# Two-part fp32r products turned into single plain fp32 products, and expert weights kept in SBUF

## The chip, the core and the metric

The kernel runs on one core of a Trainium2 chip. The core has a matrix engine (TensorE, PE in the profile, with its weight loads shown apart as PEld), VectorE (DVE), ScalarE (ACT), GpSimd (POOL), and SyncE (SP), which here only issues DMAs. The metric is the device time of one execution in microseconds (us).

## The reference, cut to what matters

x has 16 sequences of 256 tokens, each of 256 numbers. An attention layer and then a mixture of experts are added to it.

```python
xn = ln(x, g_norm); q = xn @ Wq                # 16 heads of 64
kv = xn @ Wkv                                   # one key, one value, shared by the heads
q, k = l2norm(q) * q_scale, l2norm(k) * k_scale # a null key and value stand ahead
attn = softmax(q @ k.T * 8 + relative_bias + causal + mask)
x = x + ln((attn @ v) @ Wout, g_out)
logits = (x @ wt.T + cond @ wg.T) / 2           # router over 8 experts, the best 2 weighted
y = sum over 8 experts: w[e] * ((leaky(x @ w_gate[e]) * (x @ w_up[e])) @ w_down[e])
y = y + (leaky(x @ sw_gate) * (x @ sw_up)) @ sw_down   # 2 shared blocks of 128
x = x + y
```

## The kernel before, in words

The work goes in eight rounds of 512 tokens (four tiles of 128). Round r does the attention of its tokens and, woven into it, the experts of round r - 1; after round 7 the experts of round 7 run alone. The order on every engine is written out by hand, and semaphores with counts (`need`) join the engines. Round 0 and rounds 1 to 6 (a loop) and 7 are built by the same function `attention(r, moe, following)`; in round 0 `moe` is None.

On PE a round goes like this. `turn_x1` turns the attention's output of the round before; `q_half` makes the queries (16 products of 512 columns a round, four of them ahead of time in `q_first`); `logits` makes the router's; then `gate` and `up` make 20 units of two products each (ten blocks: two shared ones and eight experts). Three of the ten blocks come before the scores, seven within them. Then 21 steps follow, each with a `score`, a `down` product of a block, a `gate` or an `up`, a `turn` of probabilities and a `value`. At the end come `turn_x` for the following round, the output product with `Wout`, and within it `keys(following)`.

Six kinds of products are made exact by parts. A number is split into a leading part, rounded to the type fp32r by a copy, and the rest, by a subtraction; `products` (lines 65 to 71) then issues three fp32r matmuls for each product of two split operands. So are made the keys' (`keys`, L1339), queries' (`q_half`, L1352), gate's and up's (`gate_up`, L1608, and in the last experts `block_half`, L1572) and the output's (with `Wout` and `oT`). The router's (`logits`, L1583) has its two weight parts side by side in one operand and two more matmuls. The other products (`down`, L1641; `score`, L1511; `value`, L1547; the null column) are plain fp32 ones already.

The parts of the activations are made in each round: ACT copies the leading part from PSUM and DVE subtracts (`keys` and `x1_parts`). The parts of the weights are made once. `Wall` (queries' and keys' columns) is split in the prologue. The gate and up weights of the ten blocks are split in round 0, one block a step from step 6 on: SP loads a block into the ring `H`, ACT makes its leading part (L740), DVE the rest (L1071), and SP writes both to an HBM scratch `wexp`. In each round all ten blocks are read again from `wexp` into `Wgu`, a ring of three blocks, by `load_weights` on SP's queue, each when the `up` that last used its place is done.

Keys' products have 256 columns, of which 144 are used (64 key, 64 value, 16 for the null key's scores): the rest are columns of the queries that stand beside them in `Wall`.

The gate and up products have one PSUM bank (`psG`) within the rounds, so a `gate` waits for DVE's `hidden` of the block before, and `up` for ACT's copy of the gate.

Of the kernel before, what the change touches and what calls it, by code (L numbers as in the profile page):

```python
# [17 lines left out]
P = 128  # L18
# [8 lines left out]
TOK = 512  # L27
# [13 lines left out]
FIRST_WEIGHTS = (1, 2, 0)  # L41
H_RING = 3
W_RING = 3
# [8 lines left out]
SPLIT_AT = 6  # L52
# [67 lines left out]
def attention_moe(nc, x, condT, condR, mask, wq, wkv, wout, wgu, wdown, wt, wgT, gnorm,  # L120
# [3 lines left out]
    wexp = nc.dram_tensor("wexp", (BLOCKS, P, 2, 2, KC, P), F32, kind="Internal")  # L124
# [4 lines left out]
    with ExitStack() as ctx:  # L129
# [13 lines left out]
        Wall = [sb(f"Wall_{part}", [P, KC, KVN + HEADS * DH], F32R) for part in PARTS]  # L143
        KV0, Q0 = 0, KVN
        WtP = sb("WtP", [P, KC, 2 * E], F32R)
        I2 = sb("I2", [2 * E, E])[:]
# [17 lines left out]
        xnT = [sb(f"xnT_{part}", [P, KC, TOK], F32R) for part in PARTS]  # L164
# [43 lines left out]
        x1T = [sb(f"x1T_{part}", [P, KC, TOK], F32R) for part in PARTS]  # L208
        Wgu = sb("Wgu", [P, W_RING, 2, 2, KC, P], F32R)
# [3 lines left out]
        LT = sb("LT", [2 * E, TOK])[:]  # L213
        WT = LT[0:E, :]
# [40 lines left out]
        wnull = misc[:, 128:160]  # L255
# [9 lines left out]
        Wq_in = work[:, 0:KC * HEADS * DH].rearrange("p (c k) -> p c k", c=KC)  # L265
# [3 lines left out]
        Wkvn_in = work[:, 4096:4096 + KC * KVN].rearrange("p (c k) -> p c k", c=KC)  # L269
# [17 lines left out]
        def logit_bank(last):  # L287

            return psY[0:2 * E, 1, :] if last else psO[0:2 * E, :]
# [41 lines left out]
        wraw_in = [events(f"wraw_in{i}", 0) for i in range(H_RING)]  # L331
        lead_done = events("lead_done", 0)
        parts_done = events("parts_done", 0)
        parts_out = [events(f"parts_out{i}", 0) for i in range(W_RING)]
# [7 lines left out]
        wgu_ld = [events(f"wgu_ld{i}", 16 * len(range(i, BLOCKS, W_RING))) for i in range(W_RING)]  # L342
# [3 lines left out]
        xnT_v = events("xnT_v", 3)  # L346
# [14 lines left out]
        x1T_v = events("x1T_v", KC)  # L361
# [16 lines left out]
        x1T_a = events("x1T_a", KC)  # L378
# [28 lines left out]
        u_ps = events("u_ps", BLOCKS, W_RING)  # L407
# [7 lines left out]
        V_MASK, V_VAR0, V_NSS, V_SILU0, V_ACT0, V_CX, V_KV, V_WALL = 2, 19, 22, 27, 29, 34, 44, 46  # L415
        V_VAR1, V_SILU1, V_ACT1, V_REL, V_RB, V_WOUT = 52, 55, 56, 58, 59, 61
# [23 lines left out]
        def _(sp):  # L440
# [6 lines left out]
            sp.dma_start(Wkvn_in[:, :, 0:2 * DH], wkv).then_inc(ld_kv.sem, 16)  # L447
# [32 lines left out]
            def load_weights(m, k):  # L480

                former = k - W_RING if k >= W_RING else max(range(k, BLOCKS, W_RING)) - BLOCKS
                need(sp, u_ps, m, former + 1)
                stand(sp, waited_sp)
                sp.dma_start(Wgu[:, k % W_RING].bitcast(F32), wexp.ap()[ORDER[k]]).then_inc(wgu_ld[k % W_RING].sem, 16)

            def experts(m):
                for k in range(W_RING, 2 * W_RING):
                    load_weights(m, k)

# [6 lines left out]
                for e in range(E):  # L497
                    if e >= WB_RING:

                        need(sp, hw_done, m, e - WB_RING + 1)  # L500
                        stand(sp, waited_sp)
                    sp.dma_start(Wb[:, e % WB_RING, :], wscr.ap()[e:e + 1, :].to_broadcast([P, TOK])) \
                        .then_inc(wb_in[e % WB_RING].sem, 16)
                    if 1 <= e <= BLOCKS - 2 * W_RING:
                        load_weights(m, 2 * W_RING + e - 1)
# [21 lines left out]
            for e in range(BLOCKS + 2):  # L527
                if e < BLOCKS:
                    if e >= H_RING:
                        sp.wait_ge(parts_done.sem, e - H_RING + 1)  # L530
                    sp.dma_start(H[:, e % H_RING, :], wgu[e].rearrange("p w c m -> p (w c m)")) \
                        .then_inc(wraw_in[e % H_RING].sem, 16)
                if e >= 2:
                    sp.wait_ge(parts_done.sem, e - 1)
                    sp.dma_start(wexp.ap()[e - 2], Wgu[:, (e - 2) % W_RING].bitcast(F32)) \
                        .then_inc(parts_out[(e - 2) % W_RING].sem, 16)
            sp.wait_ge(pre_v.sem, V_WOUT)
            sp.dma_start(xres[:], x_t[0]).then_inc(xres_in.sem, 16)
            for i in range(W_RING):
                sp.wait_ge(parts_out[i].sem, 16 * len(range(i, BLOCKS, W_RING)))  # L540
            for k in FIRST_WEIGHTS:
                load_weights(0, k)
            with sp.Fori(1, ROUNDS - 1) as r:
                load_norm_x(r + 1)
                load_round(r)
                experts(r - 1)
                for k in FIRST_WEIGHTS:
                    load_weights(r, k)
                store(r - 1)
            load_round(ROUNDS - 1)  # L550
            experts(ROUNDS - 2)
            for k in FIRST_WEIGHTS:
                load_weights(ROUNDS - 1, k)
# [80 lines left out]
        def _(act):  # L634

            act.dma_start(xin[:], x_t[0]).then_inc(xin_in.sem, 16)
            act.dma_start(Wq_in, wq).then_inc(ld_q.sem, 16)
            act.wait_ge(ld_kv.sem, 32)
            for c in range(KC):
                act.activation(Wkvn_in[:, c, 0:2 * DH], Wkvn_in[:, c, 0:2 * DH], ACT.Copy,  # L640
# [4 lines left out]
            for c in range(KC):  # L645
                act.activation(Wq_in[:, c, :], Wq_in[:, c, :], ACT.Copy, scale=gn[:, c:c + 1]) \
# [12 lines left out]
            for c in range(KC):  # L659
                act.wait_ge(w_scaled.sem, KC + c + 1)  # L660
                act.activation(Wall[0][:, c, Q0:], Wq_in[:, c, :], ACT.Copy).then_inc(w_lead.sem, 1)
            positions_turned(1)

            def keys(r, first=False):

                need(act, xnT_ps, r, 1)
                act.activation(xnT[0][:, 0, :], psT[:, 0, :], ACT.Copy).then_inc(xnT_a.sem, 1)
                if first:
                    need(act, xnT_ps, r, 2)
                    act.activation(xnT[0][:, 1, :], psT[:, 1, :], ACT.Copy).then_inc(xnT_v.sem, 1)  # L670
# [10 lines left out]
            def attention(r, moe, following):  # L681
# [35 lines left out]
                for n in range(ALL + VALUE_LAG):  # L717
# [16 lines left out]
                    if moe is None and 0 <= n - SPLIT_AT < BLOCKS:  # L734

                        e = n - SPLIT_AT
                        act.wait_ge(wraw_in[e % H_RING].sem, 16 * (e // H_RING + 1))
                        if e >= W_RING:
                            act.wait_ge(parts_out[e % W_RING].sem, 16 * (e // W_RING))
                        act.activation(Wgu[:, e % W_RING, 0], H[:, e % H_RING, :].rearrange(  # L740
                            "p (w c m) -> p w c m", w=2, c=KC), ACT.Copy).then_inc(lead_done.sem, 1)
# [36 lines left out]
            def route(m):  # L778
                for c, bank in ((0, psG), (1, psO)):
                    need(act, x1T_ps, m, c + 1)  # L780
                    act.activation(x1T[0][:, c, :], bank[:], ACT.Copy).then_inc(x1T_a.sem, 1)

            def route_half(m, half):
                for c in range(KC):
                    need(act, x1T_ps, m, KC * half + c + 1)
                    act.activation(x1T[0][:, c, half_tokens(half)], psT[:, c, half_tokens(half)], ACT.Copy) \
                        .then_inc(x1T_a.sem, 1)
# [39 lines left out]
        def _(dve):  # L827
# [69 lines left out]
            def null_columns():  # L897

                dve.wait_ge(w_scaled.sem, 2 * KC)
                for c in range(KC):  # L900
                    pre(dve.tensor_tensor(wprod, Wq_in[:, c, :].rearrange("p (h d) -> p h d", h=HEADS),
                                          knull.unsqueeze(1).to_broadcast([P, HEADS, DH]), ALU.mult))
                    pre(dve.tensor_reduce(wnull[:, c * HEADS:(c + 1) * HEADS], wprod, AX, ALU.add))
                pre(dve.tensor_copy(Wkvn_in[:, :, 2 * DH:], wnull.rearrange("p (c h) -> p c h", c=KC)))

# [827 lines left out]
```

## Time and profile before

| | |
|---|---|
| time, median of 3 runs | 1060.24 us (1060.23 to 1061.74) |
| the profiled execution: its own time | 1064.17 us |
| its span in the profile | 1062.4 us |
| mean granted TensorE clock | 0.994 |
| busy: PE, PEld | 1014.6 us (96%), 815.3 us (77%) |
| busy: DVE, ACT, POOL | 707.4, 526.5, 437.0 us |
| moved by DMA | 87.68 MB, 83 GB/s in the mean |

Busy times are of the profiled execution. The profile models the end of a matmul, and matmuls overlap in the pipe, so what one matmul costs in a row of equal ones is the distance from one start to the next, and not the duration that its row shows. In the timelines a row is: start, duration, engine, line, operation, output and inputs, shapes, count, and in brackets the idle time before it with what ended it. A shape "128*128 128x512" is that of the weights and that of the streamed operand. A plain fp32 matmul of the kernel shows as two PE instructions.

### The profile page before, as it was taken

What the parts mean: (1) busy time and instruction counts of PE and PEld (TensorE: products, weight loads), DVE (VectorE), ACT (ScalarE), POOL (GpSimd) and SP (SyncE); (2) the same over time, 40 slices, a digit from 0 to 9 for tenths busy, and PEclk for the clock granted to TensorE, in tenths of its full rate; (3) what the DMA queues carried; (4) which work ended last, traced back from release to release, by engine and by line L of the source; (5) the groups of instructions that cost most, each with busy time, mean ns of one, the idle gap of its engine ahead of it and who ended that gap; (6) DMA issues with size and microseconds to landing.
All of it is one profiled execution on the core that took longest, in us unless ns stands there. A gap on an engine that the chain in (4) does not pass through costs nothing.

```text
span 1062.4 us, 21427 instructions
## 1 busy us (share of the span) xinstructions
PE 1014.6 (96%) x6788; PEld 815.3 (77%) x6788; DVE 707.4 (67%) x2457; ACT 526.5 (50%) x1564; POOL 437.0 (41%) x422
## 2 busy tenths in 40 slices
PE   3887999999999999999999999999999999999998
PEld 2665877778777887778777787777877788777877
DVE  8789577665867558665676647676576755856543
ACT  3488346651565435663456614665246643565220
POOL 1634154441554333642535515454245534444212
PEclk9899999999999999999999999999999999999999
DMA  5316414112132013311132212311123211232043
GB/s 198 80 54 215 151 60 122 53 66 63 61 110 90 28 55 101 100 61 61 43 118 72 71 42 79 112 65 46 62 66 113 82 41 41 84 106 71 20 138 102
DMA packets 40996, 87.68 MB, mean 83 GB/s; under 512 B 4192, under 2 KB 19040, under 8 KB 40624
## 3 DMA queue, kind: packets, MB, share of 16 engines
q1 hardware_dynamic: 39920, 83.57, 24.5%
q10 hardware_dynamic: 960, 2.62, 0.7%
q8 instruction: 66, 1.08, 0.4%
q14 instruction: 50, 0.41, 0.1%
HBM read 76.57 MB, written 9.60 MB: 81 GB/s over the span
## 4 chain that ended last, share of the span: by engine, by line
PE 75%; DVE 10%; issue 5%; ACT 4%; DVEq 0%; POOL 0%; ACTq 0%
PE psY L1641 13%; PE psS L1511 6%; PE psO L1547 5%; PE psG L69 5%; PE psG L71 5%; PE psG L70 5%; PE psT L1522 5%; PE psS L71 3%; PE psS L70 3%; PE psS L69 3%; PE psS L1507 3%; PE psT L1529 2%; PE psO L1550 2%; PE psT L69 2%; PE psT L71 2%
## 5 line engine op out<-in xcount | busy, mean ns | idle before, releaser
L604 POOL TENSOR_TENSOR work<-work,rden 128x514 f32<-128x514 f32 x128 | 134.0, 1047 | 322.3 <-DVE rden L1137 321.6
L1641 PE MATMUL psY<-Wd,H 128*128 128x256 f32 x640 | 172.5, 399 | 0.0
L763 ACT ACTIVATE work<-work,low 128x257 f32<-128x257 f32 x256 | 128.5, 504 | 60.1 <-DVE low L1155 59.5
L69 PE MATMUL psG<-x1T_hi,Wgu 128*128 128x512 f32 (+1 forms) x292 | 134.8, 462 | 2.6 <-ACT leaky L807 1.9
L1641 PEld LDWEIGHTS psY<-Wd,H 128*128 128x128 f32 x640 | 112.4, 190 | 29.4 <-issue 14.4
L1155 DVE CUSTOM_DVE_ANT_0 work<-psS,bias,null_s 128x256 f32<-128x256 f32 x256 | 113.3, 480 | 28.4 <-PE psS L1511 25.9
L1251 DVE SCALAR_TENSOR_TENSOR leaky<-leaky 128x512 f32<-128x512 f32 x80 | 56.4, 704 | 101.5 <-ACT leaky L807 100.5
L71 PE MATMUL psG<-x1T_lo,Wgu 128*128 128x512 f32 (+1 forms) x292 | 114.9, 394 | 0.0
L70 PE MATMUL psG<-x1T_hi,Wgu 128*128 128x512 f32 (+1 forms) x292 | 114.4, 392 | 0.0
L593 POOL TENSOR_TENSOR rq<-qss,neghalf 128x16 f32<-128x16 f32 x32 | 97.5, 3048 | 36.3 <-DVE qss L1131 36.3
L1511 PE MATMUL psS<-KB,qT 64*128 64x256 f32 (+1 forms) x1024 | 105.7, 325 | 0.0
L1511 PEld LDWEIGHTS psS<-KB,qT 64*128 64x128 f32 x1024 | 96.8, 190 | 6.0
L767 ACT ACTIVATE work<-work,low 128x129 f32<-128x129 f32 x256 | 99.3, 390 | 0.0
L618 POOL TENSOR_TENSOR H<-H,Wb 128x512 f32<-128x512 f32 x64 | 82.1, 1283 | 37.8 <-DMA Wb<-wscr 27.7
L775 ACT ACTIVATE PTs<-psT 128x512 f32<-128x512 f32 x128 | 75.5, 590 | 40.3 <-PE psT L1522 40.3
L755 ACT ACTIVATE oT_hi<-psO 128x256 fp32r<-128x256 f32 x112 | 42.8, 382 | 101.1 <-PE psO L1550 100.2
L610 POOL TENSOR_TENSOR rstd<-ve,neghalf 128x1 f32<-128x1 f32 x32 | 17.4, 544 | 170.3 <-DVE ve L1104 170.3
L1261 DVE TENSOR_TENSOR H<-psG,leaky 128x512 f32<-128x512 f32 x75 | 51.7, 690 | 51.3 <-PE psG L71 50.1
L1522 PE MATMUL psT<-ident,work 128*128 128x128 f32 x512 | 78.1, 275 | 6.7 <-ACT PTs L775 5.9
L1522 PEld LDWEIGHTS psT<-ident,work 128*128 128x128 f32 x512 | 62.2, 141 | 24.6 <-issue 9.3
L606 POOL TENSOR_TENSOR work<-work,rden 128x258 f32<-128x258 f32 x128 | 79.3, 619 | 0.0
L1161 DVE CUSTOM_DVE_ANT_0 work<-psS,bias,null_s 128x128 f32<-128x128 f32 x256 | 79.1, 346 | 0.0
(259 smaller groups left out, 2306.7 us busy)
## 6 DMA issues: line engine op xcount, KB each, us to landing
Wgu<-wexp SPq DMA_DIRECT2D x80, 512.0 KB, 3.4
Wb<-wscr SPq DMA_DIRECT2D x64, 256.0 KB, 3.6
wexp<-Wgu SPq DMA_DIRECT2D x10, 512.0 KB, 2.9
xres<-in_x SPq DMA_DIRECT2D x8, 512.0 KB, 4.7
xin<-in_x SPq DMA_DIRECT2D x7, 512.0 KB, 4.2
out<-work SPq DMA_DIRECT2D x7, 512.0 KB, 2.9
H<-in_wgu SPq DMA_DIRECT2D x10, 256.0 KB, 3.9
bias<-bscr SPq DMA_DIRECT2D x4, 512.0 KB, 6.6
```

What stands on the lines that cost most here:

```text
L69: te.matmul(dst, a_hi, b_hi, start=start, stop=False)
L70: te.matmul(dst, a_lo, b_hi, start=False, stop=False)
L71: return te.matmul(dst, a_hi, b_lo, start=False, stop=stop)
L593: pool.tensor_tensor(rq[:, t, :], qss[:, t, :], neghalf[:], ALU.pow).then_inc(rq_done.sem, 1)
L604: pool.tensor_tensor(T1[sl][:, hs, :], T1[sl][:, hs, :], rden[sl][:, 1, hs].unsqueeze(2) .to_broadcast([P, 2, N + 1]), ALU.mult)
L618: pool.tensor_tensor(H[:, k % H_RING, :], H[:, k % H_RING, :], Wb[:, e % WB_RING, :], ALU.mult) \
L763: act.activation(T1[sl][:, h, :], T1[sl][:, h, :], ACT.Exp, scale=-1.0, bias=low[sl][:, 1, h:h + 1], accum_out=den[sl][:, 1, h:h + 1])
L767: last = act.activation(T0[sl][:, h, :], T0[sl][:, h, :], ACT.Exp, scale=-1.0, bias=low[sl][:, 0, h:h + 1], accum_out=den[sl][:, 0, h:h + 1])
L1155: ins = dve.tensor_tensor_reduce(T1[sl][:, h, 0:N], psS[:, i, 0:N], bias[:, h0 + h, :], 1.0, null_s[:, 2 * bb + 1, h0 + h:h0 + h + 1], ALU ...
L1511: mm = te.matmul(psS[:, i, first:first + keys_], qT[half, p, q1:q1 + P], KB[half, bb, 0:keys_], start=False, stop=(first == N))
L1522: mm = te.transpose(psT[:, 0, (2 * i + j) * P:(2 * i + j + 1) * P], T1[sl][:, 2 * s + i, j * P:(j + 1) * P], ident[:])
L1641: mm = te.matmul(psY[:, t // 2, (t % 2) * D:(t % 2 + 1) * D], H[:, k % H_RING, t * P:(t + 1) * P], Wd[:, ORDER[k], :], start=(k == 0 and t ...
```

## The change

- `Wall`, `xnT` and `x1T` become single fp32 tensors, and the products of keys, queries, gate, up and router become one plain fp32 matmul each for every 128 rows of the contraction. The output's product with `Wout` keeps its parts.
- Keys' products stream 144 columns in place of 256.
- The router has 8 weight columns in place of 16, and `turn_logits` adds no two halves.
- `Wgu` holds all ten blocks. SP loads them once, straight from the input, with ten DMAs of 256 KB behind the loads of the relative bias and of the next x. The splitting in round 0, the scratch `wexp`, and the 80 loads from it are gone.
- In round 0 PE waits for all ten blocks (`ld_gu`) behind the last `q_half`, ahead of the turning of the queries.
- ACT copies one half of `xnT` and `x1T` and DVE the other; the subtractions are gone.

```diff
-        Wall = [sb(f"Wall_{part}", [P, KC, KVN + HEADS * DH], F32R) for part in PARTS]
+        Wall = sb("Wall", [P, KC, KVN + HEADS * DH])
-        xnT = [sb(f"xnT_{part}", [P, KC, TOK], F32R) for part in PARTS]
+        xnT = sb("xnT", [P, KC, TOK])
-        x1T = [sb(f"x1T_{part}", [P, KC, TOK], F32R) for part in PARTS]
-        Wgu = sb("Wgu", [P, W_RING, 2, 2, KC, P], F32R)
+        x1T = sb("x1T", [P, KC, TOK])
+        Wgu = sb("Wgu", [P, BLOCKS, 2, KC, P])
...
             load_norm_x(1)
-            for e in range(BLOCKS + 2):
-                ...
+            for k in range(BLOCKS):
+                sp.dma_start(Wgu[:, k], wgu[ORDER[k]]).then_inc(ld_gu.sem, 16)
             sp.wait_ge(pre_v.sem, V_WOUT)
             sp.dma_start(xres[:], x_t[0]).then_inc(xres_in.sem, 16)
-            for i in range(W_RING):
-                sp.wait_ge(parts_out[i].sem, 16 * len(range(i, BLOCKS, W_RING)))
-            for k in FIRST_WEIGHTS:
-                load_weights(0, k)
...
                     for c in range(KC):
-                        mm = products(te, psT[:, t // 2, (t % 2) * 2 * P:(t % 2 + 1) * 2 * P],
-                                      [part[:, c, t * P:(t + 1) * P] for part in xnT],
-                                      [part[:, c, KV0:KV0 + 2 * P] for part in Wall], c == 0, c == KC - 1)
+                        mm = te.matmul(psT[:, t // 2, (t % 2) * 2 * P:(t % 2) * 2 * P + KVN],
+                                       xnT[:, c, t * P:(t + 1) * P], Wall[:, c, KV0:KV0 + KVN],
+                                       start=(c == 0), stop=(c == KC - 1))
...
-                    mm = products(te, bank[:, half, :], [part[:, c, t * P:(t + 1) * P] for part in xnT],
-                                  [part[:, c, Q0 + half * 512:Q0 + (half + 1) * 512] for part in Wall],
-                                  c == 0, c == KC - 1)
+                    mm = te.matmul(bank[:, half, :], xnT[:, c, t * P:(t + 1) * P],
+                                   Wall[:, c, Q0 + half * 512:Q0 + (half + 1) * 512], start=(c == 0), stop=(c == KC - 1))
...
                 if moe is None:
                     te.wait_ge(ld_down.sem, 16)
+                if moe is None:
+                    te.wait_ge(ld_gu.sem, 16 * BLOCKS)
                 need(te, kb_a, r, 1)
...
             def logits(m, last=False):
-                need(te, x1T_v, m, 2 * KC if last else KC)
+                need(te, x1T_a, m, 2 if last else 1)
+                need(te, x1T_v, m, 2 if last else 1)
                 for c in range(KC):
-                    te.matmul(logit_bank(last), WtP[:, c, :], x1T[0][:, c, :], start=(c == 0), stop=False, skip_group_check=True)
-                for c in range(KC):
-                    mm = te.matmul(logit_bank(last)[0:E, :], WtP[:, c, 0:E], x1T[1][:, c, :], start=False, stop=(c == KC - 1),
-                                   skip_group_check=True)
+                    mm = te.matmul(logit_bank(last), Wt[:, c, :], x1T[:, c, :], start=(c == 0), stop=(c == KC - 1))
...
             def gate_up(m, k, w, bank):
                 for c in range(KC):
-                    mm = products(te, bank, [Wgu[:, k % W_RING, part, w, c, :] for part in range(2)],
-                                  [part[:, c, :] for part in x1T], c == 0, c == KC - 1)
+                    mm = te.matmul(bank, Wgu[:, k, w, c, :], x1T[:, c, :], start=(c == 0), stop=(c == KC - 1))
...
-            def x1_parts(m):
-                for c, bank in ((0, psG), (1, psO)):
-                    need(dve, x1T_a, m, c + 1)
-                    dve.tensor_tensor(x1T[1][:, c, :], bank[:], x1T[0][:, c, :].bitcast(F32),
-                                      ALU.subtract).then_inc(x1T_v.sem, 1)
+            def x1_turned(m):
+                need(dve, x1T_ps, m, 2)
+                dve.tensor_copy(x1T[:, 1, :], psO[:]).then_inc(x1T_v.sem, 1)
```

## Rows read from the trace of the kernel before

**Rows 1.** The page's first part: busy time, share of the span, instructions

```profile
PE 1014.6 (96%) x6788; PEld 815.3 (77%) x6788; DVE 707.4 (67%) x2457; ACT 526.5 (50%) x1564; POOL 437.0 (41%) x422
```

**Rows 2.** Busy time by stretch: one round of the loop; columns: PE, PEld, DVE, ACT, POOL

```profile
365.77:491.50 125.73, 123.89 (x839) 99.52 (x838) 84.53 (x299) 63.36 (x191) 54.04 (x51) 1.00 0.23 73
```

**Rows 3.** The chain that ended last: one step of that round, and the end

```profile
423.06 1.06 PE psY L1641 x4
...
425.51 0.44 PE psT L1522 x4
...
1053.85 5.19 PE psY L1641 x24
```

**Rows 4.** Groups by line and shape: the down products and their weight loads

```profile
L1641 PE MATMUL psY<-Wd,H 128*128 128x256 f32 x640 | 172.5, 399 | 0.0
...
L1641 PEld LDWEIGHTS psY<-Wd,H 128*128 128x128 f32 x640 | 112.4, 190 | 29.4 <-issue 14.4 <-POOL H L618 1.2
```

**Rows 5.** PE's timeline: keys' products, queries' first products, the turning behind them

```profile
374.06 0.28 PE L69 MATMUL psT<-Wall_hi,xnT_hi 128*128 128x256 f32 x1
...
376.75 0.29 PE L71 MATMUL psT<-Wall_lo,xnT_hi 128*128 128x256 f32 x1
...
382.57 0.39 PE L69 MATMUL psT<-Wall_hi,xnT_hi 128*128 128x512 f32 x1
...
385.11 0.40 PE L71 MATMUL psT<-Wall_lo,xnT_hi 128*128 128x512 f32 x1
386.08 0.65 PE L1559 MATMUL psG<-ident,x 128*128 128x128 f32 x4 [0.58 <-issue]
```

**Rows 6.** PE's timeline: two of the short waits of that round

```profile
402.08 1.03 PE L1378 MATMUL psT<-ident,work 128*128 128x128 f32 x8
403.39 0.50 PE L69 MATMUL psG<-x1T_hi,Wgu 128*128 128x512 f32 x1 [0.27 <-ACT leaky L807]
...
417.02 0.40 PE L71 MATMUL psG<-x1T_lo,Wgu 128*128 128x512 f32 x1
417.89 0.34 PE L1507 MATMUL psS<-MK,pick_bf 64*128 64x384 bf16 x2 [0.47 <-DVE low L1161]
```

**Rows 7.** PE's timeline in round 0: queries turned, first, seventh and last scores

```profile
42.89 1.04 PE L1378 MATMUL psT<-ident,work 128*128 128x128 f32 x8
...
51.44 0.50 PE L1507 MATMUL psS<-MK,pick_bf 64*128 64x384 bf16 x2
...
71.82 0.34 PE L1507 MATMUL psS<-MK,pick_bf 64*128 64x384 bf16 x2
...
104.06 0.34 PE L1507 MATMUL psS<-MK,pick_bf 64*128 64x384 bf16 x2
```

**Rows 8.** SP's timeline in round 0: the relative bias out and in, weights

```profile
42.18 0.34 SPq L518 DMA_DIRECT2D bscr<-H  x1
43.78 2.04 SPq L522 DMA_DIRECT2D bias<-bscr  x4
...
46.42 2.98 SPq L531 DMA_DIRECT2D H<-in_wgu  x3
```

**Rows 9.** Busy time by stretch in round 0; last columns: clock, DMA share, GB/s

```profile
44.00:58.00 14.00, 10.82 (x52) 8.01 (x52) 9.47 (x28) 6.63 (x17) 6.16 (x2) 0.76 0.87 243
54.00:56.00 2.00, 2.00 (x17) 1.68 (x18) 2.00 (x8) 0.90 (x3) 0.00 (x0) 1.00 0.96 359
76.00:80.00 4.00, 3.29 (x34) 2.29 (x32) 3.50 (x17) 4.00 (x15) 1.99 (x4) 1.00 0.13 49
```

**Rows 10.** Groups by line and shape: the splitting of the weights

```profile
L1071 DVE TENSOR_TENSOR Wgu<-H,Wgu 128x512 fp32r<-128x512 f32 x10 | 6.8, 679 | 0.0
...
L740 ACT ACTIVATE Wgu<-H 128x512 fp32r<-128x512 f32 x10 | 6.3, 628 | 0.0
```

**Rows 11.** PE's timeline: the wait for the router in the last experts

```profile
1016.69 0.39 PE L71 MATMUL psS<-x1T_lo,Wgu 128*128 128x512 f32 x1
1018.99 0.60 PE L1605 MATMUL psT<-ident,oh 128*8 128x128 f32 x4 [1.91 <-DVE oh L1230]
```

More of the change, by code:

```diff
@@ L287, in logit_bank @@
         def logit_bank(last):
-            return psY[0:2 * E, 1, :] if last else psO[0:2 * E, :]
+            return psY[0:E, 1, :] if last else psO[0:E, :]
         def weight_bank(last):
@@ L330, in attention_moe @@
         bias_in = [events(f"bias_in{i}", 0) for i in range(BIAS_PARTS)]
[L331 to L334, printed above, removed]
+        ld_gu = events("ld_gu", 0)
         xin_in = events("xin_in", 16)
@@ L341, in attention_moe @@
         out_in = events("out_in", 16, 16)
-        wgu_ld = [events(f"wgu_ld{i}", 16 * len(range(i, BLOCKS, W_RING))) for i in range(W_RING)]
         ln_var = events("ln_var", 1)
         xn_done = events("xn_done", TILES)
-        xnT_v = events("xnT_v", 3)
+        xnT_v = events("xnT_v", 1)
         mk_done = events("mk_done", 1)
@@ L778, in route @@
             def route(m):
-                for c, bank in ((0, psG), (1, psO)):
-                    need(act, x1T_ps, m, c + 1)
-                    act.activation(x1T[0][:, c, :], bank[:], ACT.Copy).then_inc(x1T_a.sem, 1)
+                need(act, x1T_ps, m, 1)
+                act.activation(x1T[:, 0, :], psG[:], ACT.Copy).then_inc(x1T_a.sem, 1)
             def route_half(m, half):
[L784 to L787, printed above, removed]
+                need(act, x1T_ps, m, KC * half + 1)
+                act.activation(x1T[:, 0, half_tokens(half)], psT[:, 0, half_tokens(half)], ACT.Copy) \
+                    .then_inc(x1T_a.sem, 1)
             def logits(m, last=False):
@@ L976, in _, with keys @@
             null_columns()
-            kv_parts()
-            def keys(r, first=False):
+            def keys(r):
                 need(dve, xnT_ps, r, 2)
-                if first:
-                    need(dve, xnT_v, r, 1)
-                else:
-                    dve.tensor_copy(xnT[0][:, 1, :], psT[:, 1, :]).then_inc(xnT_v.sem, 1)
-                for c, ev in ((0, xnT_a), (1, xnT_v)):
-                    need(dve, ev, r, 1)
-                    dve.tensor_tensor(xnT[1][:, c, :], psT[:, c, :], xnT[0][:, c, :].bitcast(F32),
-                                      ALU.subtract).then_inc(xnT_v.sem, 1)
+                dve.tensor_copy(xnT[:, 1, :], psT[:, 1, :]).then_inc(xnT_v.sem, 1)
             def attention(r, moe, following):
@@ L1268, in sums @@
                                   ALU.add).then_inc(ysum.sem, 1)
-            keys(0, True)
-            n = [wall_trail(slice(c, c + 1), 2 * P, Q0 + HEADS * DH) for c in range(KC)]
-            assert n[-1] == V_WALL, n
             positions_second()
@@ L1578, in block_half @@
                 for c in range(KC):
[L1579 to L1580 removed]
+                    mm = te.matmul(bank[:, cols], Wgu[:, k, w, c, :], x1T[:, c, cols], start=(c == 0), stop=(c == KC - 1))
                 return mm
             def logits(m, last=False):
[L1585 removed]
+                need(te, x1T_a, m, 2 if last else 1)
+                need(te, x1T_v, m, 2 if last else 1)
                 for c in range(KC):
[L1587 to L1590 removed]
+                    mm = te.matmul(logit_bank(last), Wt[:, c, :], x1T[:, c, :], start=(c == 0), stop=(c == KC - 1))
                 mm.then_inc(lt_ps.sem, 1)
```

116 lines of the change are left out of this document (25 added, 91 removed).

## The prediction

> **What bounds the kernel now.** I read the page's busy shares first. PE stands at 96%, the next engine at 67% [rows 1], but a matmul's row is longer than what it holds the engine for, so that share alone proves nothing. The busy times by round come next: the rounds of the loop last 125.7 us each at the full granted clock, PE is busy in 123.9 of them, DVE in 84.5, ACT in 63.4, and DMA has 0.23 of its time [rows 2]. Then the chain of waits within a step of the scores: from the first `down` row at 423.06 to the turning at 425.51 it is PE behind PE, four `down` instructions of 1.06 in all and six of a gate, with no wait between [rows 3]. So in the rounds PE's own stream sets the pace, and what a product costs is the distance between starts.
>
> Two distances carry the sum. Twelve fp32r instructions of the queries start from 382.57 to 385.11 [rows 5]: 2.54 over 11 is 0.231 us for 512 columns, 0.693 for a product of three. Twenty-four of the keys start from 374.06 to 376.75 [rows 5]: 0.117 us for 256 columns. Of plain fp32 the trace has `down`: 640 instructions [rows 4], and the loops make 10 blocks x 4 tiles x 8 rounds = 320 products, so two instructions each; 24 of them in a row take 5.19 [rows 3], 0.216 each. A plain product of 256 columns is 0.432 us, where the three fp32r instructions for the same work are 0.351.
>
> **The change part by part.** *512 columns in plain fp32* is a shape that the trace does not have. If the cost follows the columns, a product is 4 x 0.216 = 0.865, that is 0.172 more than now. The bounds: no less than two instructions of 0.231 (0.462, if an instruction cost the same whatever it streams), no more than four of 0.231 (0.924). I take 0.865: `down` has the same weights, the same type and the same pairing, and the 256-column fp32r rows show at 0.117 that half the columns cost half the time, so columns set the price and not the weight loads.
>
> Queries: 8 rounds x 16 products x 0.172 = +22.0 us. Gate and up within the rounds: 7 x 40 x 0.172 = +48.2. In the last experts 32 products of 512 columns, +5.5, and 16 of 256 columns at 0.432 for 0.351, +1.3. Router: four fp32r instructions (0.924) become two products (1.73), x 8 = +6.4. Keys: 24 x 0.117 = 2.81 becomes 16 instructions of 144 columns; in the proportion of `down` that is 0.122 each, 1.94, a gain of 0.87 a round, -7.0 in all. (Four turnings of 128 columns go in 0.44 [rows 3], 0.11 each, so the weight loads allow 0.122; were keys to cost as much as 256 columns, they would lose 0.6 a round.) The work on PE: **+76.4 us**.
>
> *What the short waits swallow.* PE does stand still now and then. In the round read it had six such places: 0.74 us ahead of `turn_x1` (385.34 to 386.08 [rows 5]), 0.44 at 403.39 for ACT's copy of a gate and 0.64 at 417.89 for DVE's scores [rows 6], and three more of 0.28 to 0.40; 2.84 together. The one ahead of `turn_x1` waits for the last tile's norm while `q_first` runs; with four products of +0.172 ahead it shrinks by 0.69. The scores' waits shrink as the gate between two scores grows by 0.34 while DVE has no more to do. The waits from a gate to its `up` hold fixed work between, and stay. I take 1.9 a round, bounds 0.7 and 2.84: 7 x 1.9 = **-13.3 us**. In the last experts PE waits 2.07 for the router's choice [rows 11]; the products issued behind `turn_logits` grow by 0.8, and others ahead of a wait of 1 us: **-1.5**, bounds 0 and -3.
>
> *Parts no longer made.* Each round DVE loses two subtractions for `x1T` and two for `xnT`, ACT a copy. They lie beside queries' and output products, and DVE has a third of the round idle [rows 2]: 0 beyond the waits above. If that cover were gone, it would be some 0.7 us each.
>
> *Weights no longer read in each round.* 80 loads of 512 KB go, and DMA is idle for three quarters of a round [rows 2]. No wait of PE in the round names a DMA. The loads of the router's weights no longer queue behind weight loads on SP; PE's `down` waits for POOL 1.2 us in the whole run [rows 4]. I count 0, bounds 0 and -1.2.
>
> *The new wait in round 0.* The queries now end at 42.89 [rows 7]; with 16 products of +0.172 and the keys' gain, at 44.8. There PE now waits for the last of ten weight loads. SP issues them behind the relative bias's four loads (at 43.78 [rows 8]) and the next x; the bias needs `relative_turn`, which stands ahead of the last two products, so this starts at 45.3. Now four loads of 512 KB, x and three blocks move 3.4 MB in the 14 us from 44 to 58, 243 GB/s, with 359 GB/s in one stretch in it [rows 9]. The change makes it 5.24 MB. At 243 all is there at 66.9, at 359 from the start at 59.9; I take the present pace for the present 3.4 MB (59.5) and 359 for the 1.84 more: 64.6. Queued behind the waiting instruction are the turning of the queries, the flips of the bias and all scores, and for these wait ACT's and DVE's copies, DVE's scores and POOL. From the turning to the first score it is 8.6 us now [rows 7], some of it in waits for what will then be there; I take 6.0, as PE comes out of the pause at a low clock (0.76 in the mean of 44 to 58, where it pauses now [rows 9]). The first score then starts at 70.6, not 51.44: +19.2, of which 1.9 is in the sum already. **+17.3 us**, bounds 12.6 and 19.6.
>
> *Splitting gone.* In round 0 ACT splits a block in 0.63 and DVE in 0.68, ten times [rows 10]. These steps are ACT's: it is busy for all of 76 to 80 [rows 9], and nine steps take 32.2 us (71.82 to 104.06 [rows 7]). Between 0 and 6.8 comes back; as DVE's norm of the next x breaks two steps anyway, I take **-5**.
>
> Sum: 76.4 - 13.3 - 1.5 + 17.3 - 5 = **+73.9**. The profiled execution took 1064.17 us, 3.9 above the median of the runs, so it would take 1138, and the median 1134.
>
> **A rule beside it.** The Trainium skill's page "FP8 and Floating Point Precision", section "TensorE Precision Notes", has true fp32 as four passes through the array. The trace agrees in that a plain product of 256 columns costs 0.432, four times 0.108. Read as four of the present passes in place of three, the rule gives the first rival.
>
> **The rivals.** *Four passes, each as dear as a present one.* The 0.231 of an fp32r instruction is 0.015 above the 0.216 that `down` needs for what should be as long a stream. If 512 columns carry that surcharge in plain fp32 too, a product is 0.924, the 440 products of 512 columns cost 0.059 x 440 = 26 more: 1160. For it: the present shape has it. Against: `down` has not.
>
> *The weights cost no wait.* If the ten loads run as fast as the bias, or the pause in round 0 only moves idle time, the 17.3 go: 1117. For it: four bias loads and x came within some 12 us. Against: 2.6 MB have to follow them, and nothing else can start.
>
> *Faster: the instruction is the price.* One mechanism ends on the other side: an instruction of 512 columns costs about 0.231 whatever its type, since its weight load and hand-over set it (PEld is busy 77% [rows 1]). Then a product is 0.462, and 440 x 0.231 = 102 us come back; with the waits' and splitting's terms as above, the keys' gain, and the pause, about 960. The point from which it decides is 0.347 an instruction, half of the present product. Against it: 0.117 at 256 columns with the same weight loads, and 0.216 for `down` with as many. That the products don't become plain ones can't be: nothing else is left in the code.
>
> **How the numbers follow.** My forecast has 0.72, four dear passes 0.12, no wait for the weights 0.10, the instruction's price 0.04, else 0.02. The prediction is the likeliest, 1134. With the bounds that help (2.84 a round, 3, 12.6, 6.8) the sum is 59, 1119; with those that don't (0.7, 0, 19.6, 0) it is 91, 1151. The range takes both, and the case without a wait at 1117 with little below it: 1114 to 1154; the dear passes and the faster case lie outside with 0.16. A measurement of this kernel can't tell less than about 0.2%, 2 us, from no change. Slower 0.95, the same 0.01, faster 0.04.
>
> **What would show each step.** PE instructions fall from 6788 by about 520 (one a product, eight a round at the keys). Starts of the gate's and queries' instructions stand 0.43 apart, those of the keys 0.12. A round of the loop lasts 133 us and not 125.7. In round 0 PE stands still from about 45 to about 65, and the first score comes near 70. Scores of its later steps come less than 3.5 us apart. The wait ahead of `turn_x1` is almost gone. The prediction is wrong if 512 plain columns start 0.46 apart or 0.23, if the rounds swallow more than 3 us each, or if the weights land before the queries end.

## The result, and the profile after

The changed kernel takes **1149.13 us** (median of four runs, 1147.37 to 1150.32) where the kernel before takes 1060.24: a ratio of 1.083, 95% interval 1.081 to 1.085. It is slower by 88.9 us; forecast were 74, and 1134 us. The profiled execution takes 1150.12 us, of which the span is 1148.3.

The page's first part, to be read against [rows 1]: the matmul rows fall by exactly the 520 forecast, and PE's busy time rises by 73.5 us.

```profile
PE 1088.1 (95%) x6268; PEld 728.1 (63%) x6268; DVE 681.5 (59%) x2413; ACT 516.8 (45%) x1543; POOL 436.6 (38%) x422
```

First the new shapes. In PE's timeline of the changed kernel the keys' sixteen instructions of 144 columns start at 134.93 and the output's products behind them at 136.79: 0.116 each. Eight instructions of the queries go from 412.23 to 415.67: 0.430 each, so a plain product of 512 columns is 0.86 against 0.693 in [rows 5].

```profile
134.93 2.12 PE L1250 MATMUL psT<-Wall,xnT 128*128 128x144 f32 x16
136.79 0.38 PE L66 MATMUL psG<-Wout_hi,oT_hi 128*128 128x256 f32 x1
...
412.23 3.60 PE L1259 MATMUL psT<-Wall,xnT 128*128 128x512 f32 x8
415.67 0.27 PE L1464 MATMUL psG<-ident,x 128*128 128x128 f32 x1
418.06 0.49 PE L1464 MATMUL psG<-ident,x 128*128 128x128 f32 x3 [2.12 <-issue]
418.38 0.60 PE L1464 MATMUL psO<-ident,x 128*128 128x128 f32 x4
```

The same lines show something that no step of the prediction names. The wait *ahead* of `turn_x1` is gone, as forecast: the first transpose starts right behind the queries. But PE then stands for 2.12 us *behind the first transpose*, with "issue" as the reason: nothing that the profile shows held it. The busy times by stretch (columns as in [rows 2]) of three rounds, and of 2.4 us right behind two of these halts:

```profile
146.02:278.78 132.76, 132.76 (x773) 88.32 (x772) 81.46 (x292) 63.04 (x190) 54.01 (x51) 1.00 0.09 29
278.78:415.67 136.89, 134.32 (x774) 89.32 (x773) 82.47 (x295) 62.97 (x190) 54.02 (x51) 0.99 0.10 28
415.67:550.71 135.04, 132.92 (x774) 88.34 (x773) 82.47 (x295) 62.95 (x190) 54.01 (x51) 1.00 0.09 29
...
281.60:284.00 2.40, 2.38 (x9) 1.86 (x9) 0.69 (x1) 1.54 (x3) 0.92 (x1) 0.50 0.01 4
418.00:420.40 2.40, 2.35 (x11) 1.52 (x11) 1.41 (x4) 1.82 (x3) 1.02 (x1) 1.00 0.03 12
```

The first round of the loop takes 132.76 us, within 0.3 of the forecast 133, and PE is busy in all of it. The later five, which PE enters by branching back, take 136.89, 135.04, 137.37, 137.01 and 135.19: together 17.7 us more than five of 132.76. In these five the first two transposes start 2.4 to 3.0 us apart where the first round has 0.11. Behind the halt of 281.62 the granted clock is at its lower level, 0.50 of full speed (1.2 GHz), and the products that follow are dearer; behind that of 418.06 it stays at the upper one (2.4 GHz).

Round 0, in PE's timeline, against [rows 7]: PE stands 18.5 us at the new wait, and then turns the queries at 63.22, and the scores' first, seventh and last steps start at 68.18, 87.68 and 116.34.

```profile
42.84 1.88 PE L1259 MATMUL psS<-Wall,xnT 128*128 128x512 f32 x4
63.22 1.94 PE L1281 MATMUL psT<-ident,work 128*128 128x128 f32 x8 [18.49 <-issue]
...
68.18 0.34 PE L1412 MATMUL psS<-MK,pick_bf 64*128 64x384 bf16 x2
...
87.68 0.34 PE L1412 MATMUL psS<-MK,pick_bf 64*128 64x384 bf16 x2
...
116.34 0.34 PE L1412 MATMUL psS<-MK,pick_bf 64*128 64x384 bf16 x2
```

This wait is marked "issue" too, though the source has PE wait there for the ten loads. In the kernel with 96 increments (below) the same wait carries their name:

```profile
63.49 1.97 PE L1282 MATMUL psT<-ident,work 128*128 128x128 f32 x8 [18.62 <-DMA Wgu<-in_wgu]
```

So "issue" alone doesn't tell a wait for data from another.

In the last experts the wait for the router is 1.02 us in place of the 1.91 of [rows 11].

```profile
1101.26 0.60 PE L1506 MATMUL psT<-ident,oh 128*8 128x128 f32 x4 [1.02 <-DVE oh L1144]
```

So forecast and measurement part by 15 us, and the loop's returns hold 17.7. **Theory:** at a return PE waits for its own instructions. The page's third part counts transfers of instruction code on queue q8:

```profile
q8 instruction: 65, 1.06, 0.4%
```

These are 65 transfers of 16 KB. Nine of them fall into each round, one at 412.18, just behind the branch, and one at 415.61, where PE halts. Counting the trace's instructions on PE (each weight load, matmul, semaphore and register instruction one), the halt stands behind the sixth instruction of the loop. If a block ends there, the change, which takes matmuls and their loads out of the code ahead of the loop too (72 instructions less by that count), has put the loop's start six instructions ahead of a block's end. **Rivals:** the transposes of x1, or what they wait for, cost it; or the plain products do, dearer in their places than alone.

### The profile page after: what moved, and what is told of

It reads as the page before. It is cut to its first block, busy times and chain, and to the rows that moved or that the text cites. A ratio compares the mean times of both kernels' runs of the same rounds, so it can differ in the third digit from the quotient of the medians.

```text
span 1148.3 us, 19943 instructions
## 1 busy us (share of the span) xinstructions
PE 1088.1 (95%) x6268; PEld 728.1 (63%) x6268; DVE 681.5 (59%) x2413; ACT 516.8 (45%) x1543; POOL 436.6 (38%) x422
## 4 chain that ended last, share of the span: by engine, by line
PE 89%; DVE 2%; issue 1%; ACT 1%; POOL 0%; DVEq 0%
PE psG L1511 22%; PE psY L1540 14%; PE psS L1416 7%; PE psO L1452 5%; PE psT L1427 5%; PE psS L1259 4%; PE psT L1259 4%; PE psS L1412 3%; PE psT L1434 2%; PE psO L1455 2%; PE psT L1281 2%; PE psS L66 1%; PE psS L68 1%; PE psS L67 1%; PE psT L1250 1%
## 5 line engine op out<-in xcount | busy, mean ns | idle before, releaser
L1511 PE MATMUL psG<-x1T,Wgu 128*128 128x512 f32 x576 | 273.5, 597 | 0.0
L1511 PEld LDWEIGHTS psG<-x1T,Wgu 128*128 128x128 f32 x576 | 106.5, 190 | 92.2 <-issue 81.1
L569 POOL TENSOR_TENSOR rstd<-ve,neghalf 128x1 f32<-128x1 f32 x32 | 17.4, 545 | 165.0 <-DVE ve L1018 165.0
L1452 PE MATMUL psO<-PTs,kvs 128*64 128x256 f32 x448 | 72.7, 403 | 0.5 <-DVE oT_lo L1096 0.5
```

The lines of the kernel that those rows point to most:

```text
L1452: te.matmul(bank[i * DH:(i + 1) * DH, 0:N], kvs[:, 2 * bb, DH:2 * DH], PT[n % 2][:, i, 0:N], start=True, stop=False)
L1511: mm = te.matmul(bank, Wgu[:, k, w, c, :], x1T[:, c, :], start=(c == 0), stop=(c == KC - 1))
```

## Experiments

### Moving the loop in PE's code

Three kernels add nothing but increments of an unused semaphore, where PE stands idle in round 0 anyway: 96, 256 and 8 of them.

```
                 if moe is None:
+                    for _ in range(96):          # 256; 8
+                        te.sem_inc(spare.sem, 1)
                     te.wait_ge(ld_gu.sem, 16 * BLOCKS)
```

> The changed kernel with 96 increments of an unused semaphore on PE, put where PE waits for the weights in round 0, so that the loop's first instruction lies 96 instructions later in PE's code and all else is the same. Theory (at each return to the loop's start PE has only its first instruction in a fetched block of code and stands still until the next 16 KB arrive): the gap of 2.4 to 3.0 us behind the first transpose of turn_x1 goes, and with it the queries at a low clock after it; rounds entered by a branch fall from 135.0-137.4 to 132.8-133.5 and the whole takes 1131 to 1137 us, 12 to 18 less than 1149. Rival (the gap belongs to the transposes of x1 themselves, or to the wait that stood there before and is now later): 1148 to 1151, gaps unchanged.

> The same with 256 increments, as many as I count to a block of 16 KB: the loop's first instruction lies at the same place within its block as in the changed kernel. Theory (place within a block): the gaps stay at 2.4 to 3.0 us and the time at 1147 to 1152. Rival (any shift of the code, or the padding itself, changes the returns): like the run with 96, some 1131 to 1137. If the gap belongs to the transposes of x1, this too stays at 1149 and so does the run with 96.

> The changed kernel with 8 increments of an unused semaphore, in place of the 96, ahead of PE's wait for the weights. Counting PE's instructions in the trace, the loop's start lies six ahead of a block's end, so eight move it just past that end; the loop's 1668 instructions then lie in seven blocks and not in eight. Theory: as with 96 or better, since the padding itself takes less, 1131 to 1134, 20 transfers on PE's code queue, no gap behind the first transpose. Rival (it needs a larger shift, or 96 helped in another way): 1147 to 1150.

With 96 increments: 1133.48 us (1132.38 to 1134.34). With 8: 1133.8 (1132.01 to 1134.38). Eight instructions that do nothing take 15.3 us off. PE's timeline of the kernel with 8 at the second return, one of its rounds, and its code queue:

```profile
410.65 2.31 PE L1260 MATMUL psT<-Wall,xnT 128*128 128x512 f32 x5
412.80 0.60 PE L1467 MATMUL psG<-ident,x 128*128 128x128 f32 x4
413.24 0.60 PE L1467 MATMUL psO<-ident,x 128*128 128x128 f32 x4
...
279.97:412.73 132.76, 132.76 (x773) 88.32 (x772) 82.25 (x295) 62.96 (x190) 53.96 (x51) 1.00 0.08 28
...
q8 instruction: 20, 0.33, 0.1%
```

The eight transposes run without a gap, all six rounds take 132.77, and PE's code is transferred 20 times, not 65: past the first round the loop's code isn't fetched again at all. With 256, the halt is back at the same instruction:

```profile
432.54 0.27 PE L1467 MATMUL psG<-ident,x 128*128 128x128 f32 x1
434.69 0.49 PE L1467 MATMUL psG<-ident,x 128*128 128x128 f32 x3 [1.88 <-issue]
...
q8 instruction: 66, 1.08, 0.4%
```

That run takes 1162.55 us, outside the 1147 to 1152 expected, since 256 increments of 0.15 us last longer than the weights' wait: the first score comes at 85.59, 17.4 later. Its gaps of 2.2 to 2.4 and rounds near 134.9 are as the theory has it, the gaps a little shorter than expected. So 256 instructions are one block, the place within the block decides, and neither the transposes nor the plain products have a part in it.

### Fetched again, but entered well inside a block

```
+            for _ in range(48):                  # ahead of PE's first instruction
+                te.sem_inc(spare.sem, 1)
...
+                    for _ in range(88):          # ahead of the wait for the weights
+                        te.sem_inc(spare.sem, 1)
```

> The changed kernel with 136 increments of an unused semaphore on PE, 48 ahead of its first instruction and 88 ahead of its wait for the weights. By the count the loop then starts 130 instructions into a block and still lies in eight: it is fetched again in each round (65 or 66 transfers), but the branch finds 126 instructions in the first block. This tells apart what costs the 15 us. If it is the start just ahead of a block's end: no gap behind the first transpose, the branch back of 3.4 to 3.8 us lies under the first queries' 3.43, and the time is 1133 to 1136, as in the held cases. If it is the fetching again as such: the gaps or a wait of like size stay, 1144 to 1150.

1132.8 us (1132.22 to 1135.55), as with 8 and 96, but not for the reason tested: the loop was kept again, with 20 transfers. It reaches six instructions into an eighth block, and I had counted that as too many. With eleven kernels of this study in one table, a rule that fits all of them is another one. The start of the loop is counted in instructions within its block (placed by the halt of the changed kernel), the length in instructions; both are counts of trace records, right to two or so:

| kernel | start | length | ends after | transfers | from the last query product to `turn_x1`, at returns |
|---|---|---|---|---|---|
| before | 66 | 1803 | 1869 | 66 | 0.77 to 1.11 |
| after | 250 | 1668 | 1918 | 65 | 0.43, then a gap of 2.4 to 3.0 |
| 8 increments | 2 | 1668 | 1670 | 20 | 0.43 |
| 96 increments | 90 | 1668 | 1758 | 20 | 0.43 |
| 256 increments | 250 | 1668 | 1918 | 66 | 0.43, then 2.2 to 2.4 |
| 48 and 88 | 130 | 1668 | 1798 | 20 | 0.43 |
| gate and up alone | 66 | 1723 | 1789 | 20 | 0.23 |
| the same, shifted by 64 | 130 | 1723 | 1853 | 66 | 0.53 to 1.10 |
| queries alone | 66 | 1771 | 1837 | 66 | 0.43 |
| keys alone | 66 | 1787 | 1853 | 66 | 0.61 to 1.14 |
| keys, exact | 16 | 1764 | 1780 | 21 | 0.23 |

(Without any wait the column reads 0.43 behind a plain product and 0.23 behind an fp32r one: the product itself. The other three kernels, of the next parts, have the loops of rows above: the wait moved as "after", 65 transfers; both mendings as "96 increments", 20; the router alone as "before", 66.) Up to the first return a block's transfer starts in the traces while PE is in the block ahead of it, mostly within its first half. So a loop that ends at 1792 or a few instructions past it touches at most eight blocks with the one fetched ahead, and one that ends 45 past it touches nine. Eight are kept and nine are not. That is a count that fits these kernels and was not tested on its own; an end between 1798 and 1837 wasn't tried.

What the test was meant to tell apart, the row "queries alone" tells: there the loop is fetched again in each round, and the return costs PE nothing, because the branch's 3.3 to 3.8 us start about 1 us ahead of 3.43 us of plain queries and are over before these end. In these kernels fetching again cost 2.0 us a round and more only where the entry stands just ahead of a block's end.

### The wait for the weights, and both mendings together

```
-                if moe is None:
-                    te.wait_ge(ld_gu.sem, 16 * BLOCKS)
...
+            te.wait_ge(ld_gu.sem, 16 * BLOCKS)
             with te.Fori(1, ROUNDS - 1) as r:
```

> The changed kernel with PE's wait for the ten weight loads moved from the end of round 0's queries to the head of the loop, where their first reader stands. Prediction's term: the wait cost 17.3 in the sum, so the first score comes back from 68.2 to about 53 and the whole falls by 12 to 17, to 1132 to 1137. Rival (what PE waits for in round 0 comes about as late anyway: the bias loads, ACT's copies, POOL): less than 4 us come back, 1145 to 1149. Between them: the scores start early but the steps of round 0, which ACT and DVE set, take back a part: 1138 to 1145.

1129.00 us (1128.52 to 1129.21), 20.1 less than after. PE's timeline of this kernel: the queries are turned from 44.80 on, the next waits are those for ACT's copy and for the bias that round 0 had before, and the first score comes at 52.77, 15.4 earlier.

```profile
44.80 1.04 PE L1281 MATMUL psT<-ident,work 128*128 128x128 f32 x8
47.19 1.06 PE L1281 MATMUL psS<-ident,work 128*128 128x128 f32 x8 [1.36 <-ACT work L657]
49.21 3.64 PE L1397 MATMUL psY<-bias,flip 128*128 128x256 f32 x8 [0.95 <-DMA bias<-bscr]
52.77 0.34 PE L1410 MATMUL psS<-MK,pick_bf 64*128 64x384 bf16 x2
```

That the whole gains 20 and not 15.4 has a cause beside the wait: this kernel's five returns are milder (rounds of 134.8 to 136.6, together 5.6 us less than in the changed kernel, with the clock at its upper level behind four of the five halts). Its other runs, with a mean clock of 0.997 against 0.986 to 0.988, speak for the same; why the halts are milder there is not shown. In the sum with the loop mended that can't come in:

```
+            for _ in range(96):                  # ahead of PE's first instruction
+                te.sem_inc(spare.sem, 1)
...                                               # and the wait moved as above
```

> The changed kernel with both mendings: PE's wait for the weights at the head of the loop, and 96 increments of an unused semaphore ahead of PE's first instruction, where it stands idle. If the two losses are separate, 15.6 for the loop's code and 15.4 for the weights' wait add up: 1116 to 1120 us, all rounds of the loop 132.8, 20 transfers of instruction code on PE's queue in place of 65. If one hides the other, or the weights' loads only delay something else: 1124 to 1130. What is then left over the kernel before, 56 to 60, would be the prediction's work on PE with its short waits and splitting (76.4 - 13.3 - 1.5 - 5 = 56.6).

1116.39 us (1115.09 to 1116.44), 17.1 less than with 96 increments and the wait in its old place, and within the 1116 to 1120 expected of two separate losses. A round of this kernel, and the stretch in which the changed kernel waits:

```profile
128.35:261.12 132.77, 132.77 (x774) 88.32 (x773) 81.66 (x294) 63.05 (x190) 54.02 (x51) 1.00 0.09 29
...
43.00:69.00 26.00, 21.07 (x144) 15.89 (x144) 20.24 (x70) 18.69 (x56) 13.15 (x10) 1.00 0.64 204
```

In that stretch, which holds the ten loads, DMA moves 204 GB/s beside the scores, and PE is busy in 21.07 of 26 us, where the kernel before has 20.99. What is left over the kernel before is 55.6 us.

### The parts one at a time

Four kernels make one kind of product plain in the kernel before, with the leading parts alone, and leave all else; a fifth repeats gate and up with the loop moved by 64 increments. Queries and keys have 40 and 32 increments ahead of PE's first instruction, which keep the loop's start in its block.

```
 gate, up:  te.matmul(bank, Wgu[:, k % W_RING, 0, w, c, :].bitcast(F32), x1T[0][:, c, :].bitcast(F32), ...)
 queries:   te.matmul(bank[:, half, :], xnT[0][...].bitcast(F32), Wall[0][:, c, Q0 + ...].bitcast(F32), ...)
 keys:      te.matmul(psT[...KVN], xnT[0][...].bitcast(F32), Wall[0][:, c, KV0:KV0 + KVN].bitcast(F32), ...)
 router:    te.matmul(logit_bank(last), WtP[:, c, :].bitcast(F32), x1T[0][:, c, :].bitcast(F32), ...)
```

> The kernel before with only the gate and up products as one plain fp32 product of the leading parts; it leaves out the products with the low parts, so that its result is less exact, and keeps the weight loads of each round, the splitting and the queries as they were; the loop's first instruction keeps its place in PE's code. The prediction's terms: +48.2 in the rounds, +6.8 in the last experts, less 0.5 to 1.5 a round that short waits swallow: 1104 to 1112. Rival (the 15 us that the prediction missed come from the gate and up products being dearer in their places than alone): 1118 to 1126.

> The kernel before with gate and up in plain fp32 on their leading parts, the low parts left out, and 64 increments of an unused semaphore ahead of PE's first instruction. By my count the loop's PE code, 1723 instructions, lay in seven blocks of 256 and was fetched once (20 transfers on PE's code queue); the shift puts it across eight. Theory (eight blocks are fetched again in each round, and the branch back takes over 3 us, of which the queries' products cover all but some 0.5 to 0.8): the transfers rise to about 65, PE stands about 0.98 and not 0.23 from the last query product to the transposes of x1 at each return, as in the kernel before, and the time goes from 1099.6 to 1102 to 1105. Rival (holding the code is worth nothing here): 1099 to 1101.

> The kernel before with only the queries' products as one plain fp32 product of the leading parts, their low parts left out; 40 increments ahead of PE's first instruction keep the loop's start where it was in PE's code. At the distances read in the changed kernel (0.429 an instruction of 512 columns, 0.165 a product over the present 0.693) the 128 products cost 21. The longer first queries cover the branch back, whose 0.7 us ahead of the transposes of x1 go in each of five rounds: 17 to 19 us in all, 1077 to 1079. Rival (nothing is swallowed): 1080 to 1082.

> The kernel before with only the keys' products in plain fp32, 144 columns, on the leading parts (low parts left out); 32 increments ahead of PE's first instruction keep the loop's start where it was. The prediction's term: 0.87 a round, at the distance measured since 0.95: 7 to 7.6 us less, 1052 to 1053.5. Rival (the copies of the keys behind the products set when the queries may start, so that little comes back): 1057 to 1060.

> The kernel before with only the router's logits as two plain fp32 products of the leading parts a round, the products with the low part of x1 left out; the loop's PE code keeps its length and start. The prediction's term: four instructions of 0.231 become four of 0.429, 0.79 a round, 6.4 in all: 1065 to 1067 when nothing swallows it, 1062 to 1064 when the wait of the gates for DVE and ACT behind it takes half. Rival (the logits stand where PE has time, so that they cost nothing): 1059 to 1061. With the other parts alone (40.4, 14.8, -5.7) it should bring the sum near the 55.6 that the whole change cost without its two stalls.

| plain alone | median | over before | a round (before 125.7) | work on PE by the starts, a round |
|---|---|---|---|---|
| gate and up, code kept | 1099.62 | +39.8 | 130.3 | 40 x 0.165 = 6.6 |
| gate and up, code fetched again | 1101.18 | +40.4 | 130.7 | 6.6 |
| queries | 1075.60 | +14.8 | 127.35 | 16 x 0.165 = 2.6 |
| keys | 1055.08 | -5.7 | 124.9 | 16 x 0.116 - 2.81 = -0.95 |
| router | 1069.13 | +9.0 | 126.5 | 4 x 0.429 - 0.924 = 0.8 |

(0.165 is two plain instructions of 0.429 less three of 0.231.) Gate and up came out below both ranges, queries below the lower one, the router above all of its; keys fell between the two, and so did the shifted gate and up. The rounds say why: gate and up lose 1.6 to 2.0 of their 6.6 to waits that shrink, queries 1.0 of 2.6, keys and router nothing. The router's 0.8 a round is what was expected, 6.4 in all; its total is 2.6 above that, and no run shows why.

The two rows of gate and up also answer for the kernel before. PE's timeline at the return, code kept, and then code fetched again:

```profile
392.16 0.40 PE L71 MATMUL psT<-Wall_lo,xnT_hi 128*128 128x512 f32 x1
392.39 0.60 PE L1559 MATMUL psG<-ident,x 128*128 128x128 f32 x4
```

```profile
392.88 0.40 PE L71 MATMUL psT<-Wall_lo,xnT_hi 128*128 128x512 f32 x1
393.90 0.65 PE L1562 MATMUL psG<-ident,x 128*128 128x128 f32 x4 [0.62 <-issue]
```

The second has the wait of [rows 5], the first has none, and x, norms and queries are the same in both. In the whole the two differ by 0.6 us (39.8 and 40.4), less than their runs tell apart, so that wait is worth little.

### Keys in plain fp32, exactly, as an addition to the kernel before

Of the four parts only the keys gain. This kernel does them from an unsplit copy of the turned x (`xnP`), makes the parts that the queries need from that copy, and drops those of PE's waits that repeat one of the same round, which brings the loop's code under the limit.

```
-                act.activation(xnT[0][:, 0, :], psT[:, 0, :], ACT.Copy).then_inc(xnT_a.sem, 1)
+                act.activation(xnP[:, 0, :], psT[:, 0, :], ACT.Copy).then_inc(xnP_a.sem, 1)
+                need(act, xnP_a, r, 1)
+                act.activation(xnT[0][:, 0, :], xnP[:, 0, :], ACT.Copy).then_inc(xnT_a.sem, 1)
...
+                        mm = te.matmul(psT[:, t // 2, (t % 2) * 2 * P:(t % 2) * 2 * P + KVN],
+                                       xnP[:, c, t * P:(t + 1) * P], Wkvn_in[:, c, :], ...)
```

> The kernel before with the keys in plain fp32 from an unsplit copy of the turned x and unsplit key weights (ACT and DVE make one copy more each a round; nothing is left out), and with those of PE's waits dropped that repeat one already made in the same round. PE's loop then counts 1764 instructions and starts 16 behind a block's start, so it lies in seven blocks. Theory: the keys' products give 5.5 to 6, the held code 1.5 to 3.5 more, the copies lie beside the output products: 1051 to 1054. Rival (the copies delay the parts that the queries wait for, or DVE's norm of x1): 1055 to 1060, with a wait of PE ahead of the first queries.

1053.72 us (1052.01 to 1054.74) beside 1059.34: a ratio of 0.994, interval 0.993 to 0.995, faster than both kernels. PE's timeline has no wait at the return, nor one ahead of the queries:

```profile
246.11 2.12 PE L1362 MATMUL psT<-Wkvn,xnP 128*128 128x144 f32 x16
...
381.21 0.60 PE L1577 MATMUL psG<-ident,x 128*128 128x128 f32 x4
```

The keys give what they gave alone. That the kept code gives more is not shown: the rounds of 124.8 are those of the keys alone, so the 0.4 to 0.9 us won at a return are lost again to other waits of the round (PE is busy in 122.8 of it).

## Why the prediction was right, and where it was not

**The price of the shapes: right.** 0.429 to 0.430 an instruction of 512 columns against a forecast 0.4325, and 0.116 for 144 columns against 0.122. The four dear passes (0.462) and the price by instruction (0.231) both fall. (The 960 us of that last rival don't follow from its terms: 1060.2 - 102 - 13.3 - 1.5 - 5 - 7 + 17.3 is 949.) By the measured starts the work on PE is 21.1 + 46.2 + 6.6 + 6.3 - 7.6 = 72.6 where 76.4 was forecast.

**The short waits: right in size, one wrong in its cause.** A round should grow by 9.1 us by the measured starts (2.6 + 6.6 + 0.8 - 0.95) and grows by 7.1, from 125.7 to 132.77: 2.0 swallowed, 1.9 forecast. But the 0.74 ahead of `turn_x1` was put down to the last tile's norm. The timeline of the kernel before has that norm's product done at 384.93 (start 384.45, 0.48 long) while the last query product holds PE to 385.34. What ran until then was the branch back: the trace has it from 381.98 for 3.71 us, and 0.2 us where the code is kept. The row's own reason, "issue" and not DVE, was a hint. In the changed kernel this wait is gone as forecast, because the longer queries cover the branch: it runs from 411.19 for 3.68 us, and the last query product holds PE to 415.67. The step that failed is this reading: a wait for code was taken for a wait for data, so the sum has no term for the loop's code, and nothing in it asks where in PE's code the changed loop starts.

**What stood in its place.** The halt at the loop's second block, 15.3 to 15.7 us by the runs with 8 and with 96 increments: the whole of the difference between 1134 and 1149. The kernels that are free of it take 1133 to 1134. That 1149 still lies within 1114 to 1154 is luck: the upper end, 1151, was made of the bad ends of other terms, and none of these came out there.

**The new wait in round 0: right.** Forecast was +17.3; it cost 17.1 by the pair with the loop mended, 15.4 by the first score. The weights landed at 63.2, not 64.6, and from the turning to the first score it took 5.0, not 6.0. That the loads cost no wait (1117) is what the kernel with both mendings does, 1116.39; it was a rival for the change as it stood, and it fell there.

**Splitting gone.** The nine steps from the seventh score to the last take 28.66 us, against 32.2 in [rows 7]: 3.6 back where 5 were taken. In the whole it is only bounded: the parts alone add up to 40.4 + 14.8 + 9.0 - 5.7 = 58.5, the mended change costs 55.6, and the 2.9 between them are splitting, loads and chance together. No run took the splitting out alone.

**Weights no longer read: right.** DMA falls from 0.23 to 0.09 of a round, and nothing comes of it.

**The sum.** 55.6 + 17.1 + 15.7 = 88.4, of 88.9 measured. These are differences along one row of kernels, so they have to add up; in the other order (the wait moved first, then the loop) they are 55.6 + 12.6 + 20.1, for the milder halts of the kernel between. That the 55.6 come so near the forecast 56.6 (76.4 - 13.3 - 1.5 - 5) is in part luck: the work on PE came out 3.8 smaller, and what waits and splitting give back 2.8 smaller.

The Trainium skill's page "FP8 and Floating Point Precision", section "TensorE Precision Notes", has true fp32 as four passes. The prices fit that, with 0.86 for 512 columns, 0.215 a pass, down to 144 columns (0.232 for a product, 0.058 a pass), though no trace shows a pass by itself; so read, a pass of plain fp32 comes out below an fp32r instruction's 0.231.

## What to carry to other kernels

An idle time marked "issue" at a loop's first instructions need not be a wait for data, though it can be one: the weights' wait was marked so too. Look at the transfers of instruction code, and at where the loop starts and how much code it has, before a cause is named. An edit that only removes instructions ahead of a loop moves the loop, and here that cost a fifth of what the edit itself cost; some instructions of padding in idle time tell it apart in one run. A load that is first read in the loop is waited for there, not where its issue happens to stand.

## What the runs showed of the hardware

PE's loop code came in transfers of 16 KB, 256 instructions. By the count above, loops that touched eight such blocks, the one fetched ahead among them, were transferred once, and a return cost a branch of 0.2 us; those that touched nine were transferred again in each round (65 or 66 transfers in place of 20 or 21), and the branch took 3.3 to 3.9 us. With the first six instructions alone in the entered block, PE's first two transposes then started 2.1 to 3.0 us apart, not 0.11.

A semaphore increment took PE's queue 0.15 us.

Behind the changed kernel's halts the granted clock differed: after gaps of 2.85, 3.04 and 2.78 us it was at 1.2 GHz for some of what followed (0.50, 0.59 and 0.50 of full speed in the mean of the next 2.4 us), after 2.39 and 2.54 it stayed at 2.4 (1.00); with the wait moved, it fell once behind a gap of 2.24 (0.61). So the same halt cost 2.0 to 4.6 us a round.
